# A Mamba-2 block and a gated FFN on one core: half of the chunk transposes move from TensorE to VectorE and DMA, and the last tile's ending is re-ordered

## The reference

```python
def mamba2(xn, ...):
    zxbcdt = xn @ w_in                         # z, (x, B, C), dt
    xc = silu(causal_conv4(xbc) + conv_b)      # 768 channels
    xh, Bm, Cm = xc[:512], xc[512:640], xc[640:]
    dt = softplus(dt_raw + dt_bias); a = -dt * exp(a_log)
    u = dt[..., None] * xh                     # 8 heads of 64
    y = y_diag + y_off                         # scan over chunks, state 128 x 512
    y = y + d_skip[:, None] * xh
    return (rmsnorm(y * silu(z)) * norm_w) @ w_out
h = x + mamba2(rmsnorm(x), ...)
m = square(relu(rmsnorm(h) @ w_fc)) @ w_proj
x = layernorm(x + h + m)                       # "x1"
f = silu(lin(x, w1)) * lin(x, w2)              # 1024 wide
f = gelu(lin(f, h1)); f = gelu(lin(f, h2))     # 1024 x 1024 each
return layernorm(x + lin(f, w3))
```

## Time and profile before

| what | value |
|---|---|
| median of 3 runs | 1225.0 us |
| the profiled execution, as timed | 1225.03 us |
| its span in the trace | 1223.3 us |
| TensorE / VectorE / ScalarE / GpSimd busy | 98 / 64 / 53 / 19% |
| scan: VectorE, tenths busy in slices 4 to 16 | mostly 8 and 9 |
| mean granted TensorE clock | 0.997 |

### The profile page before, as it was taken

How to read it: one execution, slowest core, us unless ns; L and a number is a source line. 1 busy time by engine, 2 the same in 40 slices (tenths; PEclk the granted TensorE clock), 3 DMA queues, 4 the chain that set the end, 5 groups by cost and what they waited for, 6 DMA issues and landing times.

```text
span 1223.3 us, 19219 instructions
## 1 busy us (share of the span) xinstructions
PE 1196.1 (98%) x6468; PEld 1007.1 (82%) x6468; DVE 783.3 (64%) x1363; ACT 645.9 (53%) x1213; POOL 232.4 (19%) x210
## 2 busy tenths in 40 slices
PE   8899999999999999999999999999999999999996
PEld 6678888888888888788888888888888888888885
DVE  6798898989899898855535337345363363543633
ACT  6788888878788888666224124142141331422420
POOL 0517153534434261610000000000000000000000
PEclk9999999999999999999999999999999999999998
DMA  8222211222222221134500202002002020020000
GB/s 284 82 82 75 83 70 51 63 88 75 96 75 97 75 73 64 66 128 172 212 1 1 52 1 51 0 0 51 0 6 45 0 51 0 0 51 0 18 1 18
DMA packets 60696, 72.05 MB, mean 59 GB/s; under 512 B 33520, under 2 KB 52080, under 8 KB 58736
## 3 DMA queue, kind: packets, MB, share of 16 engines
q1 hardware_dynamic: 60656, 71.51, 18.0%
HBM read 63.10 MB, written 22.03 MB: 70 GB/s over the span
## 4 chain that ended last, share of the span: by engine, by line
issue 53%; POOL 0%; DVE 0%; POOLq 0%; DVEq 0%
POOL rsv_b L1885 0%; DVE o_sb L1962 0%; POOLq L1883 0%; DVEq L1716 0%; POOL rsv L235 0%; POOLq L442 0%
## 5 line engine op out<-in xcount | busy, mean ns | idle before, releaser
L1869 ACT ACTIVATE full<-bank,scale 128x512 f32<-128x512 f32 x128 | 88.3, 690 | 383.1 <-PE bank L1778 383.1
L1778 PE MATMUL bank<-hB_hi,h_sb 128*128 128x512 f32 x512 | 199.9, 390 | 0.0
L1778 PE MATMUL bank<-hB_lo,h_sb 128*128 128x512 f32 x512 | 199.7, 390 | 0.0
L1778 PE MATMUL bank<-hA_hi,h_sb 128*128 128x512 f32 x512 | 199.6, 390 | 0.0
L1778 PE MATMUL bank<-hA_lo,h_sb 128*128 128x512 f32 x512 | 199.5, 390 | 0.0
L1931 DVE CAST hA_hi<-full 128x512 fp32r<-128x512 f32 x64 | 27.4, 427 | 173.1 <-ACT full L1869 173.1
L1885 POOL TENSOR_TENSOR rsv_b<-mv_b,eps 128x4 f32<-128x4 f32 x8 | 10.7, 1342 | 618.2 <-DVE mv_b L187 618.2
L1778 PEld LDWEIGHTS bank<-hA_lo,h_sb 128*128 128x128 f32 x512 | 96.1, 188 | 20.2 <-DMA h_sb<-ffn_raw 0.2
L1778 PEld LDWEIGHTS bank<-hA_hi,h_sb 128*128 128x128 f32 x512 | 96.2, 188 | 20.0
L1778 PEld LDWEIGHTS bank<-hB_hi,h_sb 128*128 128x128 f32 x512 | 96.4, 188 | 19.1
L1778 PEld LDWEIGHTS bank<-hB_lo,h_sb 128*128 128x128 f32 x512 | 96.3, 188 | 18.9
(11 more groups left out here) (230 smaller groups left out, 2982.1 us busy)
## 6 DMA issues: line engine op xcount, KB each, us to landing
chk_xh<-w_ffn SPq DMA_DIRECT2D x16, 704.0 KB, 4.1
ffn_raw<-w_ffn SPq DMA_DIRECT2D x8, 1408.0 KB, 6.8
h_sb<-ffn_raw SPq DMA_DIRECT2D x2, 4096.0 KB, 19.4
xT<-x_t SPq DMA_DIRECT2D x8, 512.0 KB, 6.2
x_res<-x SPq DMA_DIRECT2D x8, 512.0 KB, 3.7
x_rows<-x SPq DMA_DIRECT2D x8, 512.0 KB, 3.3
x_in<-x_rows SPq DMA_DIRECT2D x8, 512.0 KB, 5.1
x_in<-x SPq DMA_DIRECT2D x7, 512.0 KB, 4.7
```

The lines of the kernel that those rows point to most:

```text
L1778: ins = pe.matmul(o, a_, b_, start=first and n == 0, stop=last and n == 1, skip_group_check=True)
L1869: nc.scalar.activation(full[:, n % FULL, :], b[:], ACT.Gelu, scale=scale[:, 1 + n // KH, n % KH:n % KH + 1]).then_inc(s_gd, 1)
```

## The change

1. **Scan, tiles 1 to 7, chunks 2 and 3.** TensorE's `turn_x` and ScalarE's `rows` are left out for them. VectorE's new `turn_squares` transposes all 32x32 squares of `xc`'s x part for both chunks in one instruction (128x1024) into `xp`, whose parts 2 and 5 are free then. SyncE stores `xp`'s parts in DRAM (512 KB), waits, and loads each chunk back in 4 DMAs of 64 KB that put the squares in their places in `xt`. GpSimd waits for those loads.
2. **SyncE's order.** The store and chunk 2's loads stand ahead of the next tile's `load_xT` and `spread_rstd`, chunk 3's loads behind them.
3. **Last FFN tile.** Blocks 5 to 7 are added a half at a time. GpSimd also forms minus mean times rstd, and ScalarE normalises the last of the four chunks; VectorE's three use add in place of subtract.

```diff
 def act_items(mlp, more):
-    order += ["xt2", "gb2", "xt3"]
+    order += ["gb2"] if mlp else ["xt2", "gb2", "xt3"]
...
+        squares = xp[:, 2::3, HALO:]
+        SQUARE_LOADS = 16 * (P // SQ)
...
+                def store_squares(i, loaded, stored):
+                    sp.wait_ge(s_sq, i)
+                    for s_l in s_late:
+                        ge(sp, s_l, loaded)
+                    sp.dma_start(sq_dram.rearrange("p (g n) -> p g n", g=2), squares).then_inc(s_sqs, 16)
+                    sp.wait_ge(s_sqs, stored)
+
+                def load_turned(n, s_free, count):
+                    c = LATE[n]
+                    sp.wait_ge(s_free, count)
+                    src = sq_dram.rearrange("(j a) (m c q b) -> c q a m j b", a=SQ, m=KI, c=len(LATE), b=SQ)
+                    for q in range(P // SQ):
+                        dst = xt[q * SQ:(q + 1) * SQ, c % 2, :].rearrange("a (m j b) -> a m j b", m=KI, b=SQ)
+                        sp.dma_start(dst, src[n][q]).then_inc(s_late[n], 16)
+
                 def tile(i, at, at_x, at_xT, at_out, piece, half, next_half):
+                    store_squares(i, loaded, stored)
+                    load_turned(0, s_u, u_made)
                     if at_xT is not None:
                         load_xT(i + 1, at_xT)
                         spread_rstd(i + 1)
+                    load_turned(1, s_skip, skip_made)
+                    if at_xT is not None:
                         sp.wait_ge(s_rsl, 16 * i + 16)
                     load_residual(i, at)
...
-                    turn_x(w, i, 2)
+                    if not mlp:
+                        turn_x(w, i, 2)
...
+                    if m in (2, 5):
+                        ge(act, s_sqs, 16 * (t - 1))
...
-                    rows(w, i, 2)
+                    if not mlp:
+                        rows(w, i, 2)
...
+                def turned_x(w, i, c):
+                    if c in LATE and w is not w_first:
+                        pool.wait_ge(s_late[LATE.index(c)], SQUARE_LOADS * i)
+                    else:
+                        pool.wait_ge(s_ad, w.act(f"xt{c}") + 1 + ACT_BANKS)
...
+                def turn_squares(t):
+                    dve.wait_ge(s_halo, t + 1)
+                    dve.wait_ge(s_xc, MC * t + MC - 1)
+                    nc.vector.transpose(squares.rearrange("p g (m n) -> p g m n", m=2),
+                                        xc[:, 0:KI, LATE[0] * P:].rearrange("p (g m) n -> p g m n", g=2)).then_inc(s_sq, 1)
...
                     mask_exponents(w, 0)
+                    if mlp:
+                        turn_squares(i)
                     mask_exponents(w, 1)
...
-                        for j in range(KH - BEHIND, KH - 2):
-                            out_rows(j)
                         for half in (range(0, CH // 2), range(CH // 2, CH)):
-                            for j in range(KH - 2, KH):
+                            for j in range(KH - BEHIND, KH):
                                 out_rows(j, half)
...
+                act.wait_ge(s_rsb, TILES + 1)
+                c = CH - 1
+                nc.scalar.activation(o_sb[:, c, :], o_sb[:, c, :], ACT.Identity, scale=rsv_b[:, c:c + 1],
+                                     bias=shift_b[:, c:c + 1]).then_inc(s_oact, 1)
...
+                pool.wait_ge(s_rsb, TILES)
+                nc.gpsimd.tensor_tensor(shift_b[:], mv_b[:, 0, :], rsv_b[:], ALU.mult).then_inc(s_rsb, 1)
```

More of the change, by code:

```diff
@@ L137, in post_ln_block @@
     PIECE = FFN_WORDS // TILES
+    SQ = 32
+    LATE = (2, 3)
     HALVES = 2
@@ L177, in layer_norm_stats, with layer_norm_tail @@
             return layer_norm_tail(step, bn, mv, eps)
-        def layer_norm_tail(step, bn, mv, eps):
+        def layer_norm_tail(step, bn, mv, eps, half=0.5):
             tt, ts = nc.vector.tensor_tensor, nc.vector.tensor_scalar
@@ L183, in layer_norm_tail @@
             step.link(tt(mv[:, 1, :], bn[:, :, 2], bn[:, :, 5], ALU.add))
-            step.mark(ts(mv[:, 0, :], mv[:, 0, :], 0.5, None, ALU.mult))
+            step.mark(ts(mv[:, 0, :], mv[:, 0, :], half, None, ALU.mult))
             step.mark(tt(mv[:, 2, :], mv[:, 2, :], mv[:, 2, :], ALU.mult))
@@ L256, in post_ln_block @@
         x1_dram = nc.dram_tensor("x1_rows", (N, D), F32, kind="Internal").ap()
+        sq_dram = nc.dram_tensor("x_squares", (P, KI * len(LATE) * P), F32, kind="Internal").ap()
         ident, ones = sb("ident", [P, P]), sb("ones", [P, P])
@@ L379, in post_ln_block @@
         flat3 = lambda ap: ap[:].rearrange("p k n -> p (k n)")
+        s_sq = sem("x_squares_turned")
+        s_sqs = sem("x_squares_stored")
+        s_late = [sem(f"turned_x_of_chunk_{c}_loaded") for c in LATE]
         s_x = sem("x_loaded")
@@ L504, in _ @@
                 load_half(2, 2 * PART)
-                def tile(i, at, at_x, at_xT, at_out, piece, half, next_half):
+                def store_squares(i, loaded, stored):
[11 more added lines that the diff above has]
+                        sp.dma_start(dst, src[n][q]).then_inc(s_late[n], 16)
+                def tile(i, at, at_x, at_xT, at_out, piece, half, next_half):
+                    kept = lambda v: v if isinstance(v, int) else sp.snap(v)
+                    loaded, stored = kept(SQUARE_LOADS * (i - 1)), kept(16 * i)
+                    u_made, skip_made = kept(CH * i + 1), kept(CH * i + 2)
+                    store_squares(i, loaded, stored)
+                    load_turned(0, s_u, u_made)
                     if at_xT is not None:
@@ L753, in iteration @@
                     exponents(w, i, 3, 0)
-                    turn_x(w, i, 3)
+                    if not mlp:
+                        turn_x(w, i, 3)
                     exponents(w, i, 3, 1)
@@ L1046, in iteration @@
                         fc_square(w, i - 1, 4)
-                    rows(w, i, 3)
+                    if not mlp:
+                        rows(w, i, 3)
                     gate_rms(step, w, i, 0)
@@ L1216, in chunk_totals @@
                     nc.gpsimd.tensor_tensor(dec[:, 2, :], dec[:, 0, :], dec[:, 1, :], ALU.mult).then_inc(s_tot, 1)
+                def turned_x(w, i, c):
[3 more added lines that the diff above has]
+                        pool.wait_ge(s_ad, w.act(f"xt{c}") + 1 + ACT_BANKS)
                 def make_u(w, i, c):
-                    pool.wait_ge(s_ad, w.act(f"xt{c}") + 1 + ACT_BANKS)
+                    turned_x(w, i, c)
                     ge(pool, s_si, CH * i + c - 1)
@@ L1679, in post_ln_block @@
         x1_in, x1_res = x_in, sb("x1_res", [P, CH, D])
-        SQ = 32
         BLOCK_LOADS = 16 * KD * (P // SQ)
@@ L1692, in post_ln_block @@
         bn_b, mv_b = sb("bn_b", [P, CH, 6]), sb("mv_b", [P, 3, CH])
-        rsv_b = sb("rsv_b", [P, CH])
+        rsv_b, shift_b = sb("rsv_b", [P, CH]), sb("shift_b", [P, CH])
         g_bank = lambda i: banks[i % B_ACT_BANKS]
@@ L1713, in post_ln_block @@
         s_o = sem("out_ready")
+        s_oact = sem("last_rows_out_ready")
         s_store = sem("out_stored")
@@ L1756, in _ @@
                     r = slice(2 * n, 2 * n + 2)
-                    sp.wait_ge(s_o, CH * i + 2 * n + 2)
+                    sp.wait_ge(s_o, CH * i + 2 + n)
+                    if n == 1:
+                        sp.wait_ge(s_oact, 1)
                     sp.dma_start(rows(out, i * TILE * D)[:, r, :], o_sb[:, r, :]).then_inc(s_store, 16)
@@ L1950, in finish_last @@
                         o = o_sb[:, r, :]
-                        dve.wait_ge(s_acc, KH * i + KH + 2 * n)
+                        dve.wait_ge(s_acc, KH * i + KH + BEHIND * n)
                         nc.vector.tensor_tensor(o, acc[n][:].rearrange("p (c n) -> p c n", c=2),
@@ L1958, in finish_last @@
                     step.wait(step.n)
-                    layer_norm_tail(step, bn_b, mv_b, EPS_LN).then_inc(s_mvb, 1)
+                    layer_norm_tail(step, bn_b, mv_b, EPS_LN, -0.5).then_inc(s_mvb, 1)
                     dve.wait_ge(s_rsb, i + 1)
-                    for c in range(CH):
+                    for c in range(CH - 1):
                         nc.vector.tensor_scalar(o_sb[:, c, :], o_sb[:, c, :], mv_b[:, 0, c:c + 1], rsv_b[:, c:c + 1],
-                                                ALU.subtract, ALU.mult).then_inc(s_o, 1)
+                                                ALU.add, ALU.mult).then_inc(s_o, 1)
                 def finish(i, more):
```

## The result

The changed kernel takes 1240.17 us, median of 4 runs (1238.18 to 1242.92), against 1225.14 for the kernel before. The ratio is 1.0117, with a 95% interval of 1.0099 to 1.0136: slower by 1.2%. The forecast was slower, at 1229.7, with a range to 1237; the time lies above both. Its profiled execution has a span of 1236.5 us, 13.2 more than before.

A forecast was written before the change was run, and what follows sets the result against it. It took TensorE's row as the tile's length, with two waits for VectorE. Tiles 2 to 6 at 5 x 1.1 = +5.5, tile 1 -0.3, tile 7 0, the end -0.5: +4.7, so 1229.7 us, range 1220.5 to 1237.

The forecast's parts named there:

- SyncE's new order: Scan, next tile's input: the reciprocals' row queues behind xT's 512 KB (1.7 us), so norm_x starts 1.1 us late.
- What bounds the tile: Scan tile: TensorE's row sets the 66.70 us length, with two places waiting for VectorE; removed transposes save 0.89 us.
- the 0.07 us at y_diag(0): Chunk 0's y_diag: TensorE's weight loads start 0.07 us after VectorE's scores end, so TensorE already waits there.
- the bank at L1430: Before the first output projection: TensorE needs the bank VectorE's addition drains by 248.30, and starts at 248.36.
- a net of nothing at the output projection: Scan tile: TensorE loses 0.9 us at y_diag(0), regains 0.36 and 0.53 by the state, if the bank were free.
- What VectorE's transpose costs: VectorE after the masks: a 1.24 us transpose moves followers by 1.17, and chunk 0's scores and y_diag by 0.9.
- The on-time case: Scan tile with all transfers in time: about 0.4 us longer, between 0 and 0.9; total 1226.2, chance 0.24.
- case C: Rival, tiles 2 to 6: norm_x starts at 247.2, 2.4 us late, total 1236.2; chance 0.18 with related cases added.
- Tile 1: Scan's tile 1: transpose hidden but for 0.3 us, 0.89 saved against the transfer chain; -0.3, between -0.9 and +0.8.
- Tile 7 and the end: Tile 7, without next input: 0, between -0.9 and +0.5; the kernel's end: together -0.5 us.
- TensorE's halves: Last FFN tile: block 5's second half goes behind block 7's first, bringing VectorE's 1212.91 to 1212.65, -0.26 us.
- ScalarE's chunk: Last FFN tile: ScalarE's 256 elements take some 0.4 us, ending with VectorE's third; -0.25, between -0.33 and +0.3.

The follow-up runs named there:

- no_turn: The changed kernel without VectorE's transpose, the squares' store and the eight loads, GpSimd not waiting (old data used): 1224.28 us, ratio 0.9987 against the kernel before.
- turn_no_dma: The changed kernel with VectorE's transpose but without the squares' store and loads, SyncE's order as before, GpSimd not waiting: 1228.31 us, ratio 1.0019.
- xt_first: The changed kernel with only xT's load moved ahead of the squares' store, the row's store staying behind chunk 2's loads: 1228.16 us, ratio 1.0021.
- tail_only: The kernel before plus only the third part of the change (last blocks by halves, last chunk normalised by ScalarE): 1225.24 us, ratio 0.9997.
- idle_slot: The changed kernel with VectorE's transpose behind x_plus_h and SyncE's order xT, squares' store, row's store and spread load, both chunks' loads: 1226.35 us, ratio 1.0001.

## Why the prediction was wrong

The direction was right and so was the chain of causes; the time of the likeliest case was short by 10 us. The step that failed is the price of SyncE's new order: norm_x was to be 1.1 us late and came 2.4 late. Beside it, tile 1 was given no part of that chain, and the clock had no term. By the prediction's own steps:

- **What bounds the tile.** Right about both places where TensorE waits for VectorE (the 0.07 us at y_diag(0), the bank at L1430). The consequence drawn was too mild: "a net of nothing at the output projection". no_turn shows that in the loop the bank alone sets it: the 0.89 us saved are worth 0.07.
- **What VectorE's transpose costs.** Its 1.24 us: right. y_diag(0) later by 0.9: measured 0.6 (237.92 less 2.55 against 234.75), half of the difference being the scores, which now lie free of GpSimd (1.20 us for 1.35). The on-time case of +0.4 a tile is +0.6 by turn_no_dma and xt_first. It was counted as though part were paid back, and none is. Nor does the transpose wait for GpSimd: it ran 1.24 us from 233.71 while GpSimd's instruction lasted from 232.85 to 234.14, which agrees with the Trainium skill (SBUF — State Buffer, Who interferes with whom: with at most one SBUF input and outside the two-port modes, no contention).
- **What SyncE's new order costs.** This is the step that failed, by size. The times against what was measured on the clock of before: end of the transpose 232.4, store issued 232.56; loads issued 235.7, 235.79; xT's issue 238.2, 238.73 (the four loads took 2.67 and 0.3 passed to xT); the row's store 238.6, 239.23; the spread load 241.7, 242.89; landed 245.6 to 245.9, 247.1. Taken one by one, the squares' store was short by 0.1, the four loads and the passage to xT by 0.44 (2.94 against 2.5), xT's issue by 0.1, the wait for the row by 0.55 (3.66 against 3.11), and the landing by 0.1. The row's wait was short because the loads ahead count too (0.7 by xt_first) and not xT alone (1.5, forecast 1.7). Together that is 1.25 us, the whole of the 1.3 kept as case C's. The tile then costs 1.7 to 2.1 and not 1.1. xt_first shows that it is this chain, and xT's place in it.
- **Tile 1.** -0.3 was wrong: its period grows by 1.5. norm_x waits 0.92 us there for the same row. That the chain applied was written down and then not added. The other two terms were off as well: the transpose was held for hidden but for 0.3 and costs 0.5 (turn_no_dma), and TensorE's 0.89 is worth 0.15 there (66.43 against 66.58 in no_turn).
- **Tile 7 and the end.** From tile 7's x_plus_h to the end of the span nothing changed in sum (721.87 against 721.92 us), where -0.5 was forecast. But it is two errors that cancel: tile 7 gained 0.8 where 0 was forecast, and what follows the scan lost 0.8. Of that 0.4 is the end, where -0.5 was forecast; the rest stays open (the kernels with the new ending take from 669.9 to 671.0 us for that stretch). Of the end's terms, TensorE's halves gave 0.17 for 0.26, ScalarE's chunk took 0.60 for 0.4 and still ended before VectorE's third; the second store, which had no term, took the gain. tail_only gives -0.1 for the end.
- **Not in the forecast.** TensorE's clock. The two spells in the profiled execution add 1.5 and 1.1 us to their tiles. The slowest run's 0.989 suggests more of them, or longer ones, but no trace shows it.

The sum as it came out in the profiled execution: 1.5 for tile 1, 9.4 for the 5 tiles after it (1.9 each), 2.5 for the clock, -0.8 for tile 7, +0.8 behind it, -0.15 ahead of the first tile, 13.2. Of the 8.5 us that the forecast's +4.7 lacked, 3.9 are the 5 tiles, 2.5 the clock, 1.8 tile 1. Without the clock that execution would have been near 1235.7, inside the range to 1237; the median lies 2 us above that execution, and its mean clock is lower (0.991 to 0.993).

Case C, given 0.18, had norm_x right (247.2, measured 247.15). That its total of 1236.2 comes near is in part luck: it charged 2.4 in each of five tiles, 12.0 for 9.4, and took 0.3 off for tile 1, which lost 1.5.

## What to carry to other kernels

An engine that is busy for 100% of a loop can still be waiting once a lap, and then work taken from it can be worth next to nothing: look at the few waits of 0.1 us, and follow the one that comes last to the engine whose row is without gaps. A DMA is charged to whoever stands behind it in the queue: before moving one, list the small latency-bound transfers that come after it, and count the bytes in front of them. Put long transfers that nobody needs yet where the issuing engine waits anyway, not ahead of a 2 KB round trip.

## What the runs showed of the hardware

- A 2 KB store to DRAM took 1.4 us from its issue to the end of the wait on an empty queue, 2.0 to 2.8 behind 256 KB in runs of 128 bytes (xt_first), and 3.5 to 3.9 behind those and 512 KB more (changed kernel). Right behind a 512 KB store it took 2.0 to 2.7 in five tiles and 3.69 in one (idle_slot).
- TensorE idle for 1.56 us in 4 was followed by about 4 us at a granted clock of 0.56 to 0.58 in tile 5, and 1.45 in 4 went with 0.53 to 0.62 in tile 6; in tiles 2 to 4, 1.48 to 1.80 us of idling did not lower it. Nor did 1.96 us early in the kernel before, where 2.54 in tail_only did (0.63). What tells them apart stays open.
- Taking an instruction from VectorE made others longer, 1.81 for 1.21 and 2.07 for 1.22 us, where they came to lie beside GpSimd's. In each the time behind the end of GpSimd's instruction is 1.1 us. VectorE's transpose, with one input, took its 1.24 us beside GpSimd as well.
